# One-hot banks of an edge-count matrix: 15 edge columns with bands of 7 destinations in place of 16 with 8

## What is computed

```
xn = layernorm(x)
x = x + gnn(xn, src, dst) + mix(xn)            # mix: linear attention, 8 heads
x = x + ffn(layernorm(x))                      # weights merged from 8 experts by a gate

# gnn
x = prelu(x @ lin_W.T + lin_b)
for l in range(2):
    agg = segment_sum(x[src], dst, n)          # sum of the source rows of each destination
    h = x + agg
    h = prelu(h @ W1[l].T + b1[l]) @ W2[l].T + b2[l]
    x = relu(batchnorm(h))
```

## Time and profile before

| | |
|---|---|
| median of 3 runs | 531.12 us (530.38 to 532.21) |
| the profiled execution, its own time | 531.56 us |
| its span, first to last instruction | 529.8 us |
| mean granted clock of PE | 0.960 of full speed |
| PE busy | 478.6 us, 90% of the span |
| DVE, ACT, POOL busy | 323.4, 251.7, 166.1 us |
| windows 0 to 24 | between 64 and 235 us |

### The profile page before, as it was taken

One profiled execution on the slowest core, in us unless ns is written; L12 is line 12 of the kernel. 1 busy time (PEld: TensorE's weight loads), 2 busy tenths in 40 slices (PEclk: granted clock), 3 DMA queues, 4 the chain that ended last, 5 costly groups with the idle time before them and its releaser, 6 DMA issues.

```text
span 529.8 us, 10016 instructions
## 1 busy us (share of the span) xinstructions
PE 478.6 (90%) x3589; PEld 363.3 (69%) x3589; DVE 323.4 (61%) x737; ACT 251.7 (48%) x526; POOL 166.1 (31%) x176
## 2 busy tenths in 40 slices
PE   2989999997997997997999995999999978989893
PEld 1767558875764665664899993668999857866641
DVE  4667698746969855863453536644333376439777
ACT  4778334137451345153235553534336377743344
POOL 1469154003039103033124990002321323303502
PEclk9989999999999989998899997999999957999998
DMA  8602001200102002002100001000000295000015
GB/s 245 188 2 79 1 12 70 81 1 29 51 2 80 2 1 79 2 6 84 74 0 0 2 1 58 1 0 1 0 0 1 83 396 240 1 0 1 1 41 153
DMA packets 5245, 27.42 MB, mean 52 GB/s; under 512 B 1036, under 2 KB 1161, under 8 KB 3544
## 3 DMA queue, kind: packets, MB, share of 16 engines
q1 hardware_dynamic: 5208, 26.92, 14.7%
HBM read 24.36 MB, written 2.56 MB: 51 GB/s over the span
## 4 chain that ended last, share of the span: by engine, by line
PE 73%; DVE 13%; ACT 9%; issue 3%; POOL 1%; DMA 1%; SPq 0%; ACTq 0%; DVEq 0%
PE ps L454 45%; PE ps L612 17%; PE ps L443 5%; PE ps L704 2%; PE ps L508 2%; DVE r L1126 1%; PE ps L440 1%; ACT wslot L756 1%; DVE r L1578 1%; PE ps L518 1%; DVE stat L1148 1%; DVE r L1590 1%; POOL late L1631 1%; DVE r L1568 1%; ACT late L864 1%
## 5 line engine op out<-in xcount | busy, mean ns | idle before, releaser
L454 PE MATMUL ps<-r,wslot 128*128 128x250 f16 x840 | 97.7, 277 | 4.4 <-DVE r L1126 4.3
L454 PEld LDWEIGHTS ps<-r,wslot 128*128 128x128 f16 x840 | 83.1, 100 | 16.9 <-DVE r L1126 5.9
L612 PE MATMUL ps<-late,r 125*128 (+1 forms) x800 | 89.7, 274 | 3.8 <-issue 3.8
L612 PEld LDWEIGHTS ps<-late,r 125*128 125x128 f16 x800 | 78.8, 99 | 15.0 <-issue 4.5
L1639 POOL TENSOR_TENSOR wslot<-stage,wslot 128x512 f16<-128x512 f32 x32 | 39.4, 1261 | 155.7 <-ACT wslot L756 155.7
L454 PE MATMUL ps<-wslot,r 128*125 128x512 f16 x300 | 69.4, 382 | 0.0
L454 PE MATMUL ps<-wslot,late 128*125 128x512 f16 x240 | 56.3, 389 | 6.3 <-DVE late L1418 5.9
L1667 POOL TENSOR_TENSOR late<-ohs,late 128x250 f16<-128x250 f32 x40 | 25.6, 651 | 99.2 <-ACT late L929 99.2
L454 PEld LDWEIGHTS ps<-wslot,r 128*125 128x125 f16 (+1 forms) x300 | 39.4, 137 | 22.2 <-issue 2.3
L454 PE MATMUL ps<-late,wslot 128*128 x480 | 51.5, 270 | 0.0
L454 PEld LDWEIGHTS ps<-wslot,late 128*125 128x125 f16 x240 | 32.8, 140 | 25.2 <-issue 7.5
(11 more groups left out here) (181 smaller groups left out, 745.3 us busy)
## 6 DMA issues: line engine op xcount, KB each, us to landing
late<-in_tv SPq DMA_DIRECT2D x2, 4096.0 KB, 17.5
x<-in_x SPq DMA_DIRECT2D x5, 448.0 KB
out<-r SPq DMA_DIRECT2D x10, 224.0 KB
stage<-in_w_up SPq DMA_DIRECT2D x2, 1024.0 KB, 5.8
stage<-in_w_down SPq DMA_DIRECT2D x2, 1024.0 KB, 4.7
stage<-in_w_lin SPq DMA_DIRECT2D x1, 1024.0 KB, 6.5
stage<-in_w_k SPq DMA_DIRECT2D x1, 1024.0 KB, 4.8
stage<-in_w_q SPq DMA_DIRECT2D x1, 1024.0 KB, 4.9
```

What stands on the lines that cost most here:

```text
L454: last = nc.tensor.matmul(out, stat_(hs, b), mov(hm, b), start=start and n == 0, stop=stop and n == 3 * blocks - 1)
L612: last = nc.tensor.matmul(bank("t", m), u_nat[layer][:, p, h, m * 128:(m + 1) * 128], counts(h)[:, chunk], start=(start and h == 0 and p = ...
```

## The change

WC goes from 16 to 15 and BAND from 8 to 7, so SPAN goes from 80 to 70. Each window has 15 matmuls of 70 columns in place of 16 of 80. `oh_s` of a window has 15 x 128 = 1920 elements on each partition (before 2048), `oh_d` has 15 x 70 = 1050 (before 1280), `rel` 150 (before 160), `base` and `offsets` 15 (before 16). `OHS` is written out in another way and stays at 6656, since other stages keep their tiles in the same memory. All line numbers behind the new one are higher by one.

```
-WC = 16
-BAND = 8
+WC = 15
+BAND = 7
 SPAN = BAND * T
...
 OH_S, OH_D = WC * 128, WC * SPAN
-OHS = 2 * (OH_S + OH_D)
+OHS = 4 * KB * CH + 5 * D + 96
+assert OHS >= 2 * (OH_S + OH_D)
...
-        oh_d = ohs[0:P, 2 * OH_S:].rearrange("p (b c n) -> p b c n", b=2, c=WC)
+        oh_d = ohs[0:P, 2 * OH_S:2 * (OH_S + OH_D)].rearrange("p (b c n) -> p b c n", b=2, c=WC)
```

## The result

The changed kernel takes 561.46 us (median of 4 runs, 557.48 to 565.23), against 531.26 for the kernel before beside it: the ratio is 1.056, with an interval of 1.049 to 1.063. It is 30 us slower, where 3.4 us faster was forecast. The profiled execution took 560.51 us, with a span of 558.7.

A forecast was written before the change was run, and what follows sets the result against it. PE was taken to bound the kernel, its windows paced by its data path, its sequencer or DVE ahead. Terms 0.75 + 0.79 + 0.56 + 0.88 + 0.38 = 3.36 us, from 531.12 to 527.8 us; range 526.3 to 529.9, 8 in 10.

The forecast's parts named there:

- (a): Windows 4 to 9, between products of `k`: paced by PE's sequencer, one register operation less in each, 6 x 0.125 = 0.75 us gained.
- (b): Windows 0 to 3: DVE paces three windows, then earlier offsets and one register operation less; 0.79 us gained, low end 0.125.
- the account of DVE and POOL shutting each other out: Windows 2, 3, 12, 13 and 14: the two engines block each other, so a shorter DVE operation also lets POOL's end earlier.
- (c): Windows 12 to 14: earlier one-hots and offsets from DVE, one register operation less; 0.56 us gained, low end 0.19.
- (e): Windows 19 and 24: offsets 0.065 and a register operation 0.125 us earlier, 0.38 us gained in all, low end 0.25.
- (d): Windows 10, 15 to 18, 20 to 23, PE's data path: fewer, narrower matmuls, 9 x 0.098 = 0.88 us gained, low end 0.32.
- rival 3: Windows' one-hot L1117 falls to one element a step, 0.42 us longer; 532.1 us, slower than before; chance 0.04.
- Rival 1: In the windows only the counts help, width gives nothing and POOL pins DVE: 1.64 to 2.6 us gained, around 529.0; chance 0.15.
- Rival 2: PE's clock: another half-clock stretch costs 1.3 us (529.1; chance 0.10), or the one behind window 19 vanishes (526.5; 0.08).
- Rival 4: A window needs 16 columns or a column 8 destinations, so the general path runs and takes milliseconds; chance 0.01.

## Why the prediction was wrong, point by point

- **The price of the load: the step that failed.** The prediction gave the load of offsets one sentence: it keeps its row, "I take nothing", and one register fewer "could give at most a sixteenth". The count of rows in the program said that nothing had moved, and I read that as "costs the same". I bounded the load below zero and not above, although its size did change, from 64 bytes to 60, and with it the place of every second one. It is 0.47 us for the remainder in 25 windows and 2.0 us for the place in 12. Of the rows at hand one bears on it, the five loads of `window_at` by DVE in the trace of before, which I took for noise:

```profile
L1095 DVEq TENSOR_LOAD <-window_at x5: 587/1181/1198, 61.0 to 191.6; - x5
```

They are of five words each, 20 bytes apart. In order of time they took 0.857, 1.198, 1.185, 1.181 and 0.587 us: the three of about 1.19 begin 20, 40 and 60 bytes on, off a 16-byte line, and the last at 80 bytes, on one. By PE's prices five words are 0.33 + 0.24 = 0.57 us from a line and 5 x 0.235 = 1.18 off it. The first, at 0.86, is on a line as well; PE's first load of offsets also takes 0.2 us more than its others (1.30 for 1.10), and no run says why.
- **How far it is passed on.** (a) had the mechanism: where the sequencer paces a window, its time is the window's. This turned against the change. Windows 6 and 7 grew by 0.35 and 2.34 us, which is 0.47 and 2.47 less the 0.125 that a register operation saves. Odd windows that had been PE's own became the sequencer's too: window 21 takes 1.74 us from its first matmul to the next product's start, before 0.58. Even ones such as windows 10 and 20 stayed PE's own, with 0.52. And not all of it arrives: window 5 passes on 2.35 us, window 21 1.59.
- **(a), the register operation.** Right. Block to block it is 5.13 to 5.23 us in the version that loads 16, before 5.25 to 5.33; and moving the load confirmed who sets the pace.
- **(b), windows 0 to 3.** Right in size together with (a): 1.39 for 1.42 us at window 8, and the count and the width come out one by one. I didn't test the account of DVE and POOL shutting each other out by an experiment; L1118 takes 1.55 us at worst and 0.71 at best, where L1117 had 1.67 and 0.83, so the worst shrank by just what the best did, 0.12 us, and that account stays open.
- **(c), (e).** Somewhat too large. In the version that loads 16, from the block behind window 11 to the one behind window 14 it is 20.70 us (156.02 to 176.72), before 21.11 (156.08 to 177.19): 0.41 us, where (c) says 0.56. From window 17's block to the context, windows 18 and 19, it is 6.57 (187.32 to 193.89), before 6.78 (188.00 to 194.78): 0.21 us, where (e) and one window of (d) say 0.29.
- **(d), the count and the width in PE's own windows.** Too large. I drew a line through 128 and 80 columns and got 0.098 us a window; 0.58 - 0.52 = 0.06 was measured. The term is about 9 x 0.06 = 0.54 us, not 0.88. The low end, 0.036 for a removed matmul and nothing for the width, was too low.
- **DVE.** Right: L1108 takes 1.149 and L1118 0.707 us, where 1.15 and 0.71 were forecast. Rows of 70 and a second buffer at 2100 bytes cost no rate, so rival 3 falls:

```profile
L1118 DVE TENSOR_TENSOR ohs<-iota,rel x25: 706/707/1551, 66.4 to 257.8; 125x1050 f16<-125x1050 f16 x25
```
- **The rivals.** None was this one. Rival 1 falls: the width did pay, 0.23 us by window 8. Rival 2 names a cost that came on top: in the profile of the changed kernel there are six half-clock stretches of 3 to 4 us between windows 1 and 19, where the profile of the kernel before has none. Its price was read too low: the context took 7.89 us, not 7.8, so 1.4 us were lost. One of the six, over PE's work behind window 7 (before: full clock):

```profile
112.00:116.00 4.00, 4.00 (x26) 2.91 (x27) 0.29 (x2) 0.68 (x2) 0.00 (x0) 0.60 0.00 0
```

Window 8, whose three products run there, grew by 1.39 us, where window 6 grew by 0.35. Five of the six begin at or behind a window (1, 7, 12, 13 and 17), and I put them down to the load's price. That is argued and not shown, since the kernel before has such stretches in some of its profiles too (152.89 for 149.88 us above). They may also be why the runs are spread from 557 to 565 us, which was not tested. Rival 4 falls by the time: a general path of milliseconds did not run.
- **The range.** It was made from errors in my own terms. None of its ends came from an operation that I had priced at nothing.

The Trainium skill has a rule that I had not looked up for this place. The page "Runtime: NRT & Kernel Launch", section "Instruction fetch mechanics", gives such a load about 200 ns a register "even for bulk"; the page means loads whose words come from HBM. Here the words lie in SBUF: the rule comes near the loads off a line (0.235 us a word) and not those on one (0.26 us for four).

## What to carry to other kernels

A size that shrinks also moves whatever is laid out behind it: when a count goes from 16 to 15, list every buffer whose stride is made from it and see who reads it, the sequencers' register loads first. Keep a small table that a sequencer loads at whole groups of four words from a 16-byte line, even if some words are not used. An operation that isn't counted as busy, such as a load to registers, needs a price with both ends in the sum, since where a sequencer paces the work it costs its full time. And when two profiles are compared by position, count from a place that the change can't have touched.

## What was not expected of the hardware

- A register load from SBUF costs 0.26 us for each four words from a 16-byte line, and 0.235 to 0.24 for each single word, whether in the remainder or off the line: 16 words take 1.10 us on it and 3.81 off it. DVE's loads of five words fit the same prices (0.587 on a line, 1.18 to 1.20 off it).
- While the output was being stored, with the DMA engines busy for 0.6 to 0.98 of the time, loads took up to twice as long, whole groups too: 4 words 0.66 us for 0.33, 16 words 2.16 for 1.10, 15 words 2.76 for 1.58.
- A window matmul seems to take its time by the 16-byte lines of its moving rows, read from one profile each: 0.036, 0.034, 0.032 and 0.029 us for 80 columns, 70 in unaligned rows, 70 in aligned rows, and 60.
